# K, V and the queries of chunks 0 and 1 made inside the scan loop of a Mamba, attention and mixture-of-experts decoder layer, kept in DRAM and loaded under the tail

## The reference, cut to what matters

```python
x = x + mamba_block_and_ffn(layernorm(x))        # selective scan over 2048 tokens
x = x + cross_attention(layernorm(x), ctx)       # 16 heads of 16, 1601 keys
x = x + soft_moe(layernorm(x))                   # 8 experts, 128 slots each

# the scan: 512 channels, 16 states each
dA = exp(d_t[..., None] * A)
h  = dA * h + (d_t * u_t)[..., None] * b_t[:, None, :]
y  = einsum('bdn,bn->bd', h, c_t)

# the attention
q = split_heads(x @ Wq + bq); k = split_heads(y @ Wk + bk); v = split_heads(y @ Wv + bv)
out = softmax(q k^T / 4) v @ Wo + bo
```

## Time and profile before

| | us |
|---|---|
| median of 3 runs | 1644.81 (1643.01 to 1645.91) |
| the profiled execution, its own time | 1639.34 |
| its span in the trace | 1637.5 |
| mean granted TensorE clock | 0.902 of full speed |
| busy: PE, DVE, ACT, POOL | 1359.1, 770.3, 913.6, 406.7 |
| steps 0 to 127 of the scan loop | 49.5 to 652.6 |
| first score matmul | 879.0 |

### The profile page before, as it was taken

The page is one execution under the profiler, slowest core; times in us unless marked ns, Lnnn a source line. Parts: engine busy times, 40 slices in busy tenths (PEclk is TensorE's granted clock), DMA queues, the critical chain, the costliest instruction groups (busy, mean ns, idle before and its releaser), DMA issues.

```text
span 1637.5 us, 15369 instructions
## 1 busy us (share of the span) xinstructions
PE 1359.1 (83%) x5571; PEld 642.8 (39%) x5571; DVE 770.3 (47%) x845; ACT 913.6 (56%) x1268; POOL 406.7 (25%) x290
## 2 busy tenths in 40 slices
PE   6477578787888859897725999999999988979999
PEld 2122134353434424554521223223223234558887
DVE  3899989979997998205610001001001016561011
ACT  4536445655574436012425997998998954760310
POOL 0556655554565564104130000000000001000000
PEclk9779888899899979879756999999999988989999
DMA  5323332332233232201994000000000000010801
GB/s 190 112 80 138 121 108 95 130 103 90 90 130 103 103 128 90 53 0 39 107 108 48 1 1 1 1 1 0 0 0 0 0 0 1 1 52 17 343 13 39
DMA packets 35631, 107.95 MB, mean 66 GB/s; under 512 B 3650, under 2 KB 14146, under 8 KB 32915
## 3 DMA queue, kind: packets, MB, share of 16 engines
q1 hardware_dynamic: 35572, 107.19, 23.3%
HBM read 93.60 MB, written 2.36 MB: 59 GB/s over the span
## 4 chain that ended last, share of the span: by engine, by line
PE 49%; DVE 21%; ACT 16%; issue 8%; DMA 5%; SPq 2%; POOL 0%; DVEq 0%; ACTq 0%; POOLq 0%
DVE ps L904 11%; PE ps L1591 10%; PE ps L1576 9%; ACT arena L739 6%; PE ps L1395 4%; PE ps L1700 4%; PE ps L1350 3%; DMA arena<-arena 3%; PE ps L1741 3%; DVE arena L915 3%; ACT ps L595 2%; PE ps L1729 2%; PE ps L1281 2%; PE ps L1718 2%; PE ps L1295 1%
## 5 line engine op out<-in xcount | busy, mean ns | idle before, releaser
L739 ACT ACTIVATE arena<-ps,bound 128x1024 f32<-128x1024 f32 (+1 forms) x416 | 420.8, 1213 | 26.3 <-PE ps L1576 26.2
L439 POOL TENSOR_TENSOR arena<-arena 128x1024 f32<-128x1024 f32 x128 | 300.6, 2349 | 250.3 <-DVE arena L915 212.9
L904 DVE TENSOR_TENSOR_SCAN ps<-ps,arena 128x1024 f32<-128x1024 f32 x128 | 300.7, 2349 | 25.8 <-ACT ps L595 15.7
L1350 PE MATMUL ps<-arena,ident 128*128 128x512 f32 x512 | 255.7, 641 | 56.8 <-DVE arena L915 56.7
L1576 PE MATMUL ps<-arena 97*128 (+3 forms) x832 | 218.7, 385 | 21.9 <-issue 19.8
L1591 PE MATMUL ps<-arena 128*32 128x512 f32 (+1 forms) x1664 | 222.5, 607 | 1.1 <-ACT arena L739 0.9
L595 ACT ACTIVATE ps<-arena 128x512 f32<-128x512 f32 x256 | 166.2, 682 | 66.8 <-DVE arena L915 62.9
L426 POOL TENSOR_TENSOR rstd<-ve,mhalf 128x4 f32<-128x4 f32 (+3 forms) x18 | 23.4, 1302 | 632.5 <-DVE ve L1199 468.2
L1350 PEld LDWEIGHTS ps<-arena,ident 128*128 128x128 f32 x512 | 100.1, 203 | 200.0 <-issue 110.4
L1174 DVE COPY arena<-ps 128x512 f32<-128x512 f32 x16 | 11.1, 692 | 354.1 <-PE ps L1591 354.1
L915 DVE TENSOR_TENSOR arena<-ps,arena 128x1024 f32<-128x1024 f32 x128 | 156.0, 1219 | 6.8 <-DVE ps L904 0.5
(11 more groups left out here) (182 smaller groups left out, 1468.3 us busy)
## 6 DMA issues: line engine op xcount, KB each, us to landing
arena<-bc_scratch SPq DMA_DIRECT2D x128, 512.0 KB, 4.0
arena<-in_mw SPq DMA_DIRECT2D x16, 1024.0 KB, 9.6
arena<-arena SPq DMA_DIRECT2D x48, 128.0 KB, 14.8
arena<-arena SPq DMA_DIRECT2D x12, 400.2 KB, 16.7
arena<-in_w SPq DMA_DIRECT2D x2, 1024.0 KB
out<-xt SPq DMA_DIRECT2D x4, 512.0 KB, 2.9
xt<-in_x SPq DMA_DIRECT2D x1, 1536.0 KB
arena<-in_ctx SPq DMA_DIRECT2D x1, 1200.8 KB, 7.6
```

The source lines that it names most:

```text
L439: pool.tensor_tensor(dbu[:, w % DR], du[:, DP * p:DP * p + DP], over(bg[:, w // BG % 2, n % BG], DP), ALU.mult).then_inc(S["dbu_ready"], 1)
L739: act.activation(flat(prob[0:n, v % 2, 2 * h:2 * h + 2]), ps[0:n, 2 * (r % 3):2 * (r % 3) + 2, :].rearrange("p a b -> p (a b)"), ACT.Exp, ...
L904: dve.tensor_tensor_scan(decay_banks(w), decay_banks(w), flat(dbu[:, w % DR]), carry[:, DP * p, n:n + 1], ALU.mult, ALU.add).then_inc(S["s ...
L1350: last = mm(bank(x), ident[:, :], state(2 * j + s)[:, x], start=False, stop=(j % HP == HP - 1 and (j in SUMMED or s == 1)))
```

## The change

K and V, in four pieces of up to 512 keys and seven of up to 256 rows, are made and split in chunk 0 of the scan loop (the last parts in chunk 1), and the queries of chunks 0 and 1 in chunk 3. Their parts go to three DRAM tensors `kx_d`, `vx_d` and `qx_d`, in 48 stores for K (36 of 1 KB a row, 12 of 130 bytes), 7 for V and 24 for the queries; 5 small stores put the rows of ones and zeros there. In the loop the subtractions are on GpSimd (`key_rest`, `query_rest`) and the bias, copies and squares on ScalarE. The layout of the loop is turned round so that `kx` and the first half of `qx` lie over what is dead after the last scan: `vx` is loaded at step 28 of chunk 3, `kx` (4.9 MB) and two chunks of `qx` (1.6 MB each) when the last state is added. `wout`, `w1` and `w2` are loaded after K and V have left, in chunk 1. The queries of chunks 2 and 3 are made in the tail, up to their lengths; their split (now all on VectorE) and their way through DRAM come behind the bound, and TensorE waits for them behind the attention of chunk 0. In chunk 3 the hidden layer of chunk 2 stands two steps earlier and its second product one step, and the last `gated` stands ahead of `second_residual`.

The diff, cut:

```diff
+K_MARKS = [["kf", "kf", "kp0", "ksq", "kp1", "kp2", "lengths"]] * 3 + [["kf", "kf", "kp0", "ksq", "kp1", "lengths", "kp2"]]
...
+            def store_keys(j, n):
+                o, w = KCOLS[j]
+                sp.wait_ge(S["k_act"], k_count(j, "kp%d" % n))
+                for r, (_, b) in enumerate(TERMS):
+                    if b == n:
+                        for k in range(DK):
+                            sp.dma_start(kx_d[HD * r:HD * r + HD, HALF * k:HALF * k + HALF, o:o + w],
+                                         kp[n][:, k, 0:w]).then_inc(S["kx_out"], 16)
...
+            def load_ffn():
+                sp.wait_ge(S["vx_out"], 16 * len(VPAIRS))
+                sp.wait_ge(S["kx_out"], 16 * KSENT * len(KCOLS))
...
+            def keys_and_values_out(q):
+                if q in (4, 9, 12):
+                    store_keys((4, 9, 12).index(q), 0)
...
+                if q in (14, 15, 16):
+                    store_values(2 * q - 28)
+                    store_values(2 * q - 27)
...
+                if q == 19:
+                    load_ffn()
...
             for c in range(NC):
                 sp.wait_ge(S["bc_stored"], c * 16 + 16)
                 for i in range(NS):
...
+                    keys_and_values_out(c * NS + i)
+                    if c == NC - 1:
+                        queries_out(i)
...
-            sp.wait_ge(S["yz_ready"], NC * DP)
+            sp.wait_ge(S["y_acc"], NC * NP)
+            sp.dma_start(kx[0:XR], kx_d[0:XR, :, :]).then_inc(S["kx_in"], 16)
+            load_queries(0)
+            load_queries(1)
...
+            def key_rest(j, n):
+                pool.wait_ge(S["k_act"], k_count(j, "kp1" if n else "ksq"))
+                w = KCOLS[j][1]
+                pool.tensor_tensor(kf[:, :, 0:w], kf[:, :, 0:w], kp[n][:, :, 0:w], ALU.subtract).then_inc(S["kr_ready"], 1)
...
                     scan_input(w)
+                    if c == 0 and i in (3, 13, 21):
+                        key_rest((3, 13, 21).index(i), 0)
+                    if c == 0 and i in (6, 16, 23):
+                        key_rest((6, 16, 23).index(i), 1)
...
+                        if i in (2, 12, 20, 31):
+                            key_parts((2, 12, 20, 31).index(i))
+                        if i in (5, 15, 22):
+                            key_part((5, 15, 22).index(i), 1)
...
+                if c == NC - 1:
+                    if i in (0, 8):
+                        query_stats(i // 8)
+                    if i in (1, 9):
+                        query_variance(i // 9)
+                    if i in (4, 12):
+                        normed_query(i // 12)
...
+                if i == 19:
+                    pe.wait_ge(S["xdbl_ready"], 2)
+                    pe.wait_ge(S["k_act"], k_count(1, "lengths"))
+                    keys(2)
...
+            pe.wait_ge(S["kx_in"], 16 * 5)
             pe.wait_ge(S["bound_ready"], 1)
```

More of the change, by code:

```diff
@@ L190, in decoder_layer @@
-        region = a.at
[L192 to L204, removed]
-        qp = [a2.take(2, DK * C, dt=BF16) for _ in range(3)]
+        k0 = Stack(gate_at)
@@ new lines, in decoder_layer @@
+        ctxt = k0.take(2, KV)
+        wk = k0.take(2, DM)
+        assert k0.at <= w1_at
+        wv = Stack(h1t_at).take(2, DM)
+        kf = Stack(hsum_at).take(DK, 512)
+        ksq = Stack(h1_at).take(DK, 512)
+        k1 = Stack(w2_at)
+        kp = [k1.take(DK, 512, dt=BF16) for _ in range(3)]
+        zero_row = k1.take(C, dt=BF16)
+        one_row = Stack(hsum_at).take(KV, dt=BF16)
+        k2 = Stack(w1_at)
+        vst = [k2.take(2, NH, 2 * HD), k2.take(2, NH, 2 * HD), Stack(wout_at).take(2, NH, 2 * HD)]
@@ L714, in _ @@
[L714 to L724 removed]
+            turned_query(3)
@@ new lines, in values @@
+            def values(v):
+                b0, nb = VPAIRS[v]
+                for b in range(b0, b0 + nb):
+                    n = min(P, KV - b * P)
+                    acc = work(1)[0:n, P:P + DM] if nb == 1 else work(v)[0:n, part(b - b0)]
+                    for x in range(2):
+                        mm(acc, ctxt[0:CP, x, b * P:b * P + n], wv[0:CP, x], start=(x == 0), stop=False)
+                    last = mm(acc, ones[0:1, 0:n], rows[0:1, 1, :], start=False, stop=True)
+                last.then_inc(S["v_ps"], 1)
@@ new lines, in query_lengths, with queries @@
+            def query_lengths(c):
+                pe.wait_ge(S["q_act"], q_count(c, "qsq"))
+                for i in range(CT):
+                    for k in range(DK):
+                        at_col = i * NH + k * HALF
+                        last = mm(ps[:, 7 if c < 2 else 2, at_col:at_col + HALF], xat[c][:, k, tok(i)], sel[:, :], start=True, stop=True)
+                last.then_inc(S["qn_ps"], 1)
+            def queries(i):
+                if i == 5:
+                    pe.wait_ge(S["sp_in"], NC * DB)
+                    turn_query(0)
+                if i == 7:
+                    project_query(0)
+                if i == 13:
+                    pe.wait_ge(S["hsum_ready"], 2 * (NC - 1))
+                    query_lengths(0)
+                if i == 14:
+                    pe.wait_ge(S["q_act"], q_count(0, "lengths"))
+                    turn_query(1)
+                if i == 16:
+                    project_query(1)
+                if i == 18:
+                    query_lengths(1)
```

711 lines of the change are left out of this document (441 added, 270 removed).

## The result

The changed kernel takes **1545.43 us** (median of 4 runs, 1544.89 to 1545.59) beside 1643.91 for the kernel before: ratio 0.9399, 95% interval 0.9383 to 0.9415, or 98.5 us less. In a later job the same kernel gave 1543.82 (5 runs) and 0.9402 (0.9387 to 0.9417). The forecast was 1541, with 1530 to 1555 for its own case.

A forecast was written before the change was run, and what follows sets the result against it. VectorE was taken to bound the scan loop, ScalarE and TensorE attention, and a chain the stretch between. 120.5 + 6.2 - 22.6 = 104 us less gave 1535 for the profiled execution, 1541 as a median, range 1530 to 1555.

The forecast's parts named there:

- What leaves the tail: Stretch between scan loop and attention: first score at 758.5 instead of 879.0 before the other terms, 120.5 us less.
- rival 3: Before attention: kx and qx arrive late, TensorE waits 49 us longer, time 1590; chance 4 in 100.
- The end of chunk 3: TensorE's additions, hidden layer and second products run with hardly a wait, output projection not behind `gated`: 6.2 us less.
- Steps 0 to 8: Chunk 0: 0.4 us at the start, and 4.7 at steps 3 to 7 from GpSimd's subtractions delaying scan inputs.
- Steps 19 to 22: Chunk 0: third piece of K holds ScalarE, then GpSimd, then the scan of step 22; 7.6 us more, the costliest.
- Steps 12 to 18: Chunk 0: VectorE's convolution gives cover; bounds nothing and 4.7 us, 2 us more taken.
- the new scalings: VectorE's two added sets of four scalings, counted at 1.4 us each; waiting out GpSimd's products by the port rule: 4.7 more.
- The queue: SyncE's list in the loop: 84 stores and three loads between the B and C loads; 2 us more taken.
- Chunk 3: VectorE's statistics and scaling for the queries, first 2.1 us covered at step 2: 4.9 more, plus 1 for GpSimd's waits.
- the first: Rival for the loop: waits do not stay apart and the loop pays much more, time 1569; chance 23 in 100.
- the second: Rival for SyncE's queue: stores delay each B load, 5 us for each of 24 groups, time 1657; chance 2 in 100.

The follow-up runs named there:

- rest2_late: Changed kernel with GpSimd subtracting the first part of K's third piece behind the input of step 22, not ahead; profiled span 1537.4 us beside 1543.1.
- no_rest: Changed kernel without GpSimd's eight subtractions of K and its waits for ScalarE there (second and third parts wrong); ratio 0.9287 to the kernel before.
- double: Changed kernel with each store of K and of the queries issued twice, the second to an unread DRAM tensor; span 1550.2 us beside 1543.1.
- v_late: Changed kernel with V's stores, K's last stores and the output and feed-forward weights' load one group of two steps later; ratio 0.9399 to the kernel before.
- keys_early: Changed kernel with K's third piece made ahead of the second skip in chunk 0, ScalarE's related work one step earlier; ratio 0.9368 to the kernel before.
- lengths_early: Changed kernel with ScalarE copying the lengths of K's third piece at step 23, not step 24; ratio 0.9370 to the kernel before.
- q2_late: Changed kernel with chunk 2's split queries stored only after ScalarE's first four exponentials of attention; profiled span 1536.3 us beside 1543.1.

## Why the prediction came out as it did

**What leaves the tail** held step by step. From the output projection to the first score it was 78.3 us for a forecast of 80.5: the loads of kx, qx and vx were in (TensorE waited for none of them, rival 3), the projection took 4.9 for 5.1, lengths 1.97 for 3.6. The loads took longer than the 23 us that I had worked out from 360 GB/s: 8.4 MB came from 699.6 to about 741, some 200 GB/s, and were in 42 us ahead of the first score. One term was too small: "1.2 us follow before the first score". The kernel before shows the gap behind a wait of 16.96 us for the stores; there the engine's instructions may have come in under that wait. Behind a bound that comes last it is 3.7.

**The end of chunk 3**: 6.2 us forecast, 7.4 measured (26.4 against 33.8), and the order is worth 10.5 in all: the old one pays a slower clock behind its stop as well. 1.7 us of that is the output projection (8.83 against 7.17), which the tail above counts as its own.

**Steps 0 to 8**: 5.1 forecast, 5.9 measured, of them 0.9 at the start. The waits of 1.0 and 3.5 us for GpSimd at steps 4 and 7 are the ones that were worked out (1.4 and 3.3).

**Steps 19 to 22**: 7.6 forecast, 10.0 measured. The mechanism was the one written; the term "makes the third piece of K from 152.7 to 154.5" was half its size. A piece of K is 8 records, as an addition is, 3.6 us and not 1.8; and the addition ahead of it took 4.7 with part of it at the low clock and not 3.65. What I had left out is that the piece holds ScalarE's decays back as well (rest2_late: 5.9 us of wait with GpSimd out of the way).

**Steps 12 to 18**: 2 forecast; in steps 9 to 17 it was 4.2, and none of it as a wait. Three instructions of VectorE got longer. Kernel before, then after, there with GpSimd's products beside the last two:

```profile
88.47 1.40 DVE L870 TENSOR_TENSOR arena<-arena 128x1024 f32<-128x1024 f32 x1
...
120.92 0.28 DVE L854 COPY arena<-arena 128x12 f32<-128x12 f32 x1
...
133.23 0.19 DVE L826 TENSOR_SCALAR ve<-mv 128x4 f32<-128x4 f32 x1
```

```profile
94.41 2.72 DVE L1074 TENSOR_TENSOR arena<-arena 128x1024 f32<-128x1024 f32 x1
...
128.10 1.20 DVE L1058 COPY arena<-arena 128x12 f32<-128x12 f32 x1
...
141.32 2.28 DVE L1030 TENSOR_SCALAR ve<-mv 128x4 f32<-128x4 f32 x1
...
126.93 2.35 POOL L562 TENSOR_TENSOR arena<-arena 128x1024 f32<-128x1024 f32 x1
...
141.22 2.35 POOL L562 TENSOR_TENSOR arena<-arena 128x1024 f32<-128x1024 f32 x1
```

They are old instructions; GpSimd's subtractions shifted its products onto them. The copy and the small scaling end where GpSimd's product does, at 129.3 and 143.6, and in no_rest, where the products stand elsewhere, the three took 1.40, 0.28 and 0.20. In the prediction I used the port only for the new scalings. Those of chunk 3 took 1.38 and 3.11, so the 1.4 for each was 1.7 short once. By the Trainium skill, "SBUF — State Buffer", section "Who interferes with whom", a VectorE operation with two inputs in SBUF contends with GpSimd's reads too, not only the forms with a 2-port mode; the trace agrees: 2.72 for the tensor_tensor, 2.56 for one scalar_tensor_tensor, while the product with C, which reads PSUM, took 1.20 to 1.23 throughout.

**The queue: 2 forecast, 8.1 measured.** This is the step that failed. I had looked for stores that take long, and found them cheap, rightly (double: 4.8 us at most for 72 more). I had not asked who makes what a store waits for. SyncE stood 20.2 us for V's copies, behind ScalarE, behind a TensorE at half the clock. The clock's share of the 8.1 is not exact: with V made at the full clock steps 30 to 36 still cost 0 to 5 us. No row of before could show that clock, but the earlier trace rows has 0.92 in the loop, so stretches of it were there.

**Chunk 3**: 5.9 forecast, 5.2 measured (28.6 to 33.8), the first statistics hidden at step 2 as written.

**The sum.** The loop paid 11.2 more, the end of chunk 3 gave 1.2 more, the tail 2.1 more, and 1.9 were lost behind the first score: the profiled execution took 1544.89 where 1535 was forecast. That the median came out at 1545.4 and so only 4.4 above the forecast is partly chance: I added 5.5 us for the profiled execution of before lying below its median, and after's lies 0.5 below.

Of the rivals the first had the right direction (the waits do not stay apart), and its price of 28 was too high. The time of the second was added up wrongly: 1541 with 120 for the 2 of the queue is 1659 and not 1657.

## What to carry to other kernels

When work is moved into a loop, follow each new piece from its producer to the last one who waits in order, and price the producer first: here one late piece of TensorE stood behind the waits of ScalarE, GpSimd, VectorE and SyncE, and the profile names the last of them. Removing the wait that the profile names gave nothing one or two steps on (v_late, rest2_late), changing the order at its source 5 us each time (keys_early, lengths_early; in the first about half of it through TensorE's clock), and the parts together 11. After that look at what the engines now do at the same time: a filled gap put GpSimd beside VectorE's scalings and took 3.9 of 9.6 us.

## What the hardware did that I had not expected

- A short stop of TensorE can cost more than its length. Behind a stop of 2.4 us the clock was 0.50 to 0.55 for 12 us (188 to 200), behind one of 4.7 us 16 products took 6.50 for 3.62 us, behind one of 1.2 us (lengths_early) it was 0.50 from 188 to 196. q2_late fell to 0.57 in the middle of full work, so I give no rule.
- The pattern of that clock was the same in two profiles of one program (and its mean 0.924 or 0.925 in all 9 runs), and different in the one profile of another with the same loop (q2_late), by 8 us at the loop's end. A difference of that size between two kernels wants the windows of the clock before an explanation.
- A branch that jumps over some 300 matmuls took 3.7 to 4.2 us until the next matmul (twelve profiles) and 0.65 with the body left out. By the Trainium skill, "Runtime: NRT & Kernel Launch", section "Instruction fetch mechanics", a taken branch to a target outside the fetched pages waits for a fetch; the trace agrees: a fetch of 16 KB lies in the gap, and none with the body left out.
- VectorE's smallest instructions can take as long as a large one: 128x4 elements took 2.28 us beside GpSimd's product and 0.19 without it.
